# Cross-attention and quantised FFN on one core: two PSUM banks moved between the weighted values and the chunks, and all four engine orders rewritten

## The reference

```python
# x: 32 x 256 x 256, side and ctx: 32 x 256 x 256, mask: 32 x 16 x 256 x 256
z = layernorm(x)
k = concat(side @ Wk.T + bk, ctx @ Wgk.T + bgk)     # 512 keys
v = concat(side @ Wv.T + bv, ctx @ Wgv.T + bgv)
q = z @ Wq.T + bq                                   # 16 heads of 64
att = softmax(where(mask, -inf, q k' / 8))          # the mask covers the first 256 keys
x = x + (att @ v) @ Wo.T + bo
y = layernorm(x) / s_in -> bf16 -> float8 e4m3 -> @ quantised kernel * scales -> bf16 + bias
out = x + y
```

## Time and profile before

| | |
|---|---|
| runs | 2736.74, 2736.12, 2734.57 us |
| profiled execution, its own time | 2734.6 us |
| its span, first to last instruction | 2732.8 us |
| mean granted TensorE clock | 0.995 of full |
| TensorE busy | 2677.5 us (98%) |
| VectorE busy | 2163.6 us (79%) |
| GpSimd busy | 2048.8 us (75%) |
| ScalarE busy | 1859.6 us (68%) |
| chain that ended last | TensorE 80%, ScalarE 7%, issue 6%, VectorE 5% |
| HBM traffic | 74.8 MB, mean 27 GB/s |

### The profile page before, as it was taken

The page is one execution under the profiler, slowest core; times in us unless marked ns, Lnnn a source line. Parts: engine busy times, 40 slices in busy tenths (PEclk is TensorE's granted clock), DMA queues, the critical chain, the costliest instruction groups (busy, mean ns, idle before and its releaser), DMA issues.

```text
span 2732.8 us, 66539 instructions
## 1 busy us (share of the span) xinstructions
PE 2677.5 (98%) x20352; PEld 2349.6 (86%) x20352; DVE 2163.6 (79%) x5329; ACT 1859.6 (68%) x4454; POOL 2048.8 (75%) x2503
## 2 busy tenths in 40 slices
PE   5999999999999999999999999999999999999996
PEld 4888888888888888888888888888888888888885
DVE  5888777888778887778877788887788877788875
ACT  4766667766667666677666676666776666776664
POOL 4787777877777877777877778777788777787774
PEclk9999999999999999999999999999999999999998
DMA  3000000001000000000000000000000100000100
GB/s 144 24 24 24 27 27 23 27 19 31 23 27 27 27 19 27 27 23 27 19 31 23 27 27 27 19 27 27 26 24 19 31 27 24 26 27 19 31 16 8
DMA packets 57246, 75.18 MB, mean 28 GB/s; under 512 B 4992, under 2 KB 39296, under 8 KB 57216
## 3 DMA queue, kind: packets, MB, share of 16 engines
q1 hardware_dynamic: 57216, 74.81, 9.0%
HBM read 66.40 MB, written 8.39 MB: 27 GB/s over the span
## 4 chain that ended last, share of the span: by engine, by line
PE 80%; ACT 7%; issue 6%; DVE 5%; DMA 0%; SPq 0%; POOL 0%; DVEq 0%; ACTq 0%; POOLq 0%
PE ps_misc L603 28%; PE ps_scores L685 15%; PE ps_o L712 15%; PE ps_pt L697 13%; PE ps_misc L653 8%; ACT probs L875 3%; DVE probs L1144 2%; ACT pt_hi L882 2%; DVE pt_lo L1155 2%; ACT kv_out L852 1%; DVE o_t L1163 1%; PE ps_misc L662 1%; PE ps_misc L632 0%; DMA probs<-wv_t_dram 0%; ACT q_hi L840 0%
## 5 line engine op out<-in xcount | busy, mean ns | idle before, releaser
L477 POOL TENSOR_SCALAR probs<-probs,recips 128x512 f32<-128x512 f32 x1024 | 729.7, 723 | 330.2 <-DVE recips L1151 324.2
L875 ACT ACTIVATE probs<-probs,neg_max 128x512 f32<-128x512 f32 x1024 | 739.7, 725 | 214.8 <-DVE neg_max L1144 205.4
L1144 DVE CUSTOM_DVE_ANT_1 probs<-ps_scores,mask_sb 128x512 f32<-128x512 f32 x960 | 636.2, 685 | 217.9 <-PE ps_scores L685 177.6
L882 ACT CAST pt_hi<-ps_pt 128x512 fp32r<-128x512 f32 x1024 | 565.6, 589 | 306.7 <-PE ps_pt L697 300.0
L1155 DVE TENSOR_TENSOR pt_lo<-ps_pt,pt_hi 128x512 fp32r<-128x512 f32 x1024 | 675.6, 683 | 108.1 <-ACT pt_hi L882 107.0
L697 PE MATMUL ps_pt<-ident,probs 128*128 128x128 f32 x4096 | 554.2, 274 | 6.1 <-POOL probs L477 3.7
L712 PE MATMUL ps_o<-pt_hi,v_hl 128*128 128x256 f32 x2048 | 548.6, 302 | 3.0 <-DVE pt_lo L1155 3.0
L712 PE MATMUL ps_o<-pt_lo,v_hl 128*128 128x256 f32 x2048 | 508.1, 282 | 0.0
L697 PEld LDWEIGHTS ps_pt<-ident,probs 128*128 128x128 f32 x4096 | 457.3, 141 | 46.8 <-issue 35.5
L712 PEld LDWEIGHTS ps_o<-pt_hi,v_hl 128*128 128x128 f32 x2048 | 387.0, 189 | 62.0 <-issue 58.0
L712 PEld LDWEIGHTS ps_o<-pt_lo,v_hl 128*128 128x128 f32 x2048 | 389.3, 190 | 0.0
(11 more groups left out here) (105 smaller groups left out, 5846.1 us busy)
## 6 DMA issues: line engine op xcount, KB each, us to landing
mask_sb<-mask_dram SPq DMA_DIRECT2D x128, 256.0 KB, 3.1
x_sb<-x_dram SPq DMA_DIRECT2D x32, 256.0 KB, 2.7
side_raw<-side_t_dram SPq DMA_DIRECT2D x32, 256.0 KB, 3.8
scr_b<-ctx_t_dram SPq DMA_DIRECT2D x32, 256.0 KB, 2.7
out_dram<-y SPq DMA_DIRECT2D x32, 256.0 KB, 2.1
probs<-wq_t_dram SPq DMA_DIRECT2D x1, 1024.0 KB, 5.0
o_t<-wk_t_dram SPq DMA_DIRECT2D x1, 1024.0 KB, 7.3
wo_sb<-wgk_t_dram SPq DMA_DIRECT2D x1, 1024.0 KB, 9.3
```

The source lines that it names most:

```text
L477: nc.gpsimd.tensor_scalar(p, p, recips[:, h % RING, t:t + 1], 1.0, ALU.mult, ALU.mult).then_inc(norm_done, 1)
L875: nc.scalar.activation(p, p, ACT.Exp, bias=neg_max[:, h % RING, t:t + 1], scale=-1.0, accum_out=sums[:, h % RING, t:t + 1]).then_inc(exp_d ...
L882: nc.scalar.copy(pt_hi[:, h % 2, 2 * k:2 * k + 2, :], ps_pt[:, k, :, :]).then_inc(pthi_done, 1)
L1144: V.tensor_tensor_reduce(out=p, in0=s, in1=mask_sb[:, row::MASK_ROWS - row, :], scale=MASK_STEP, scalar=SCORE_LIMIT, op0=ALU.add, op1=ALU.min,
```

## The change

The weighted values get one bank, the chunks three; the wait of outputs moves from the add of the last head but one to that of the last head. GpSimd's semaphore for the split of the side and context rows becomes two, one for each. The four lists are rewritten: each has the same steps as before (TensorE 89, ScalarE 95, VectorE 122, GpSimd 72) in another order. SyncE's list is the same.

```diff
-MISC_BANKS = 2
+MISC_BANKS = 3
...
-        ps_o = psum("ps_o", [P, 2, 512])
+        ps_o = psum("ps_o", [P, 512])
...
-                if some(c.head(h) - 1):
-                    pe.wait_ge(o_done, c.head(h) - 1)
+                if some(c.head(h)):
+                    pe.wait_ge(o_done, c.head(h))
...
-                        last = mm(ps_o[:, h % 2, 0:S], v_hl[:, n % 2, kt, i, :], pt[:, h % 2, kt, :],
+                        last = mm(ps_o[:, 0:S], v_hl[:, n % 2, kt, i, :], pt[:, h % 2, kt, :],
...
-                    nc.scalar.copy(o_lo[:], ps_o[DK:P, h % 2, 0:S]).then_inc(olo_done, 1)
+                    nc.scalar.copy(o_lo[:], ps_o[DK:P, 0:S]).then_inc(olo_done, 1)
...
-                    V.tensor_tensor(dst, ps_o[0:DK, e, 0:S], o_lo[:], ALU.add).then_inc(o_done, 1)
+                    V.tensor_tensor(dst, ps_o[0:DK, 0:S], o_lo[:], ALU.add).then_inc(o_done, 1)
```

More of the change, by code:

```diff
@@ L438, in split_rows @@
                 wait_apart(pool, "pool", loaded, 16 * n)
-                nc.gpsimd.tensor_scalar(kv_hi[:, :, keys], raw, 1.0, 0.0, ALU.mult, ALU.add).then_inc(kvhi_done, 1)
-                pool.wait_ge(kvhi_done, 2 * (n - 1) + part + 1)
+                nc.gpsimd.tensor_scalar(kv_hi[:, :, keys], raw, 1.0, 0.0, ALU.mult, ALU.add).then_inc(kvhi_done[part], 1)
+                pool.wait_ge(kvhi_done[part], n)
                 nc.gpsimd.tensor_tensor(kv_lo[:, :, keys], raw, kv_hi[:, :, keys].bitcast(F32),
@@ L756, in batch @@
                 outputs(c, 3)
-                transposes(c, 4, 0)
-                transposes(c, 4, 1)
+                transposes(c, 5, 0)
+                transposes(c, 5, 1)
                 chunk(c, "v0", 2)
                 chunk(c, "k1", 2)
-                transposes(c, 5, 0)
+                chunk(c, "v1", 2)
+                outputs(c, 4)
+                chunk(c, "q", 3)
                 scores(c, 8, 0)
[L763 to L766, removed]
+                outputs(c, 5)
                 transposes(c, 6, 0)
                 transposes(c, 6, 1)
-                chunk(c, "q", 3)
                 chunk(c, "k0", 3)
+                scores(c, 8, 1)
+                chunk(c, "xq_prev", 0)
+                chunk(c, "k1", 3)
                 transposes(c, 7, 0)
-                outputs(c, 5)
                 transposes(c, 7, 1)
@@ L790, in batch @@
                 transposes(c, 10, 0)
+                outputs(c, 9)
                 transposes(c, 10, 1)
-                outputs(c, 9)
                 scores(c, 12, 1)
@@ L795, in batch @@
                 transposes(c, 11, 0)
+                outputs(c, 10)
+                scores(c, 14, 0)
                 transposes(c, 11, 1)
-                scores(c, 14, 0)
-                outputs(c, 10)
                 chunk(c, "k0", 0)
@@ L807, in batch @@
                 outputs(c, 12)
+                chunk(c, "k1", 0)
                 scores(c, 16, 0)
-                chunk(c, "k1", 0)
+                outputs(c, 13)
                 transposes(c, 14, 0)
@@ L813, in batch @@
                 scores(c, 16, 1)
-                outputs(c, 13)
+                transposes(c, 15, 0)
                 outputs(c, 14)
-                transposes(c, 15, 0)
                 transposes(c, 15, 1)
@@ L1225, in batch @@
-                attended(c, 0)
                 mins(c, 4, 0)
                 mins(c, 5, 0)
+                o_adds(c, 0)
+                pt_los(c, 1, 1)
+                attended(c, 1)
+                mins(c, 4, 1)
+                recip(c, 3)
                 pt_los(c, 2, 0)
                 pt_los(c, 2, 1)
-                attended(c, 1)
+                o_adds(c, 1)
+                mins(c, 5, 1)
                 moments_y(c)
-                mins(c, 4, 1)
-                o_adds(c, 0)
-                mins(c, 5, 1)
+                split_los(c, "q", 2)
```

243 lines of the change are left out of this document (120 added, 123 removed).

## The result

| | before | after |
|---|---|---|
| median us | 2735.69 (4 runs, 2734.57 to 2736.74) | 2768.65 (4 runs, 2766.69 to 2769.93) |
| ratio | 1 | 1.0120, 95% interval 1.0102 to 1.0137 |
| profiled execution, own time | 2734.6 | 2769.8 |

The change makes the kernel slower by 33 us, 1.2%. I had forecast slower by 12; the measured time lies just outside my range.

A forecast was written before the change was run, and what follows sets the result against it. TensorE was taken as the bound in all 30 middle batches. 82.81 + 0.82 + 0.10 = 83.73 us a batch against 83.34, +0.4 in each of 30, 12 us: median 2736.1 to 2748, range 2731 to 2768.

The forecast's parts named there:

- TensorE's bare steps, 82.81 a batch: TensorE's steps in the new order, laid end to end without waits, would take 82.81 us a batch.
- the 0.10 that I kept: TensorE's many stalls of 0.01 us, 0.10 a batch before the change, were assumed to stay.
- Transposes (12, 1) and outputs 11 behind scores (14, 0) have 0.1 to spare.: On TensorE around heads 11 to 14, these steps would not be late, with 0.1 us of slack.
- The third bank: Chunk-end-to-refill distance would be 2.6 us at the batch's first chunk, over 3.7 elsewhere; the bank wins 0.07 at most.
- All of these cost nothing: Moves in other queues, including the residual copy 15 us later, would cost nothing, with cover of 5 us or more.
- GpSimd and VectorE stretch each other here and there by 0.4, which my spacings leave out.: Said in support of the rival that the single bank costs at more places; stretches of 0.4 us were not counted.
- The place where one values bank fails, 0.82: Between scores (8, 1) and (10, 1), outputs 7 would be 0.51 us late and scores (10, 1) 0.82 in all.
- my lower bound of 0.4: Least cost between scores (8, 1) and (10, 1), from VectorE's own work never waiting for ScalarE: 0.4 us late.
- The rule on rotating banks: Skill's rule, speaking against one values bank; forecast held that other steps cover the evacuation in 15 of 16 heads.
- The third: Rival: single bank costs at more places, two of heads 5, 7, 9, 13 losing 0.4 each: 2772 us; chance 0.15.
- the forecast chain: ScalarE's row, then VectorE's add, reciprocal and minima, delaying scores (10, 1) by 0.82 us a batch, bounds 0.4 to 1.2.

The follow-up runs named there:

- best3: mins14_copyx_kvlo with head 6's lower copy before exp (9, 1), reciprocal 9 behind minimum (11, 0), GpSimd's rstd and head 9's second normalisation earlier: 2723.81 us.
- nocopyx: mins14_copyx_kvlo with GpSimd's residual copy put back where the changed kernel has it, behind head 7's first normalisation: 2745.45 us.
- mins14_copyx_kvlo: Changed kernel with head 14's first minimum and exp later, residual copy behind head 4's normalisation, v0 2's low part behind head 7's second normalisation: 2736.53 us.
- chain_short_norm9: mins14_copyx_kvlo with head 6's lower copy before exp (9, 1), x's moments and reciprocal 9 later, head 9's second normalisation earlier: 2749.30 us.
- copyx_early: Changed kernel with only GpSimd's residual copy moved, from behind head 6's normalisation to behind head 4's: 2759.36 us.
- old_banks: Changed kernel's new orders with the old bank numbers, two for the weighted values and two for the chunks: 3086.11 us.

## Why the prediction was wrong

- *TensorE's bare steps, 82.81 a batch.* Held, within about 0.2: best3 comes to 83.03 with no step more than about 0.05 late. The small stalls come to 0.22 there and 0.12 in the changed kernel, against the 0.10 that I kept.
- *"Transposes (12, 1) and outputs 11 behind scores (14, 0) have 0.1 to spare."* **This step failed**, by 0.71 a batch, nearly half of the 1.55 that stands where I had laid out nothing. I laid out the minimum of (14, 0) at 1.16 after its scores, and did not ask what else it waits for. I had looked at the waits that the diff edits, and not at those of the ring of four, whose text is unchanged but whose release (transposes (11, 1)) the new list moves behind its user. VectorE stands idle for 2.28 us just there, so its share of busy time would not have shown this wait.
- *The third bank: "over 3.7 at all others", and "wins 0.07 at most".* **Failed.** I measured the distance from a chunk's end to the refill of its bank; for q 3 to k1 3 it is over 5 us. What counts is when VectorE's list reaches the emptying: behind the quantising, the copy of v1 2 and the add of head 5. The wait is 0.66. As the prediction itself put it, TensorE would not be seen waiting for a chunk's bank; it is, 32 times.
- *"All of these cost nothing" (the residual copy moved by 15 us).* **Failed.** I followed its DMAs and SyncE's queue, where it indeed costs nothing, and left out the copy's own time on GpSimd, put into a stretch in which that engine has hardly a hole (94% busy from 1340 to 1356): 1.5 us of work, which the meetings with VectorE's quantising steps make 2.8. nocopyx prices it at 9 us once the other waits are gone; in the changed kernel it shows as 0.20 at transposes 8 and as a part (0.33) of the wait of k1 3, and these overlap, so they are not to be added to other prices.
- *"GpSimd and VectorE stretch each other here and there by 0.4, which my spacings leave out."* Left out wrongly: one such stretch, 0.6 longer than in the kernel before, was what made q's low part late.
- *The place where one values bank fails, 0.82.* The chain exists, step by step, but was mis-sized: 0.45 in mins14_copyx_kvlo, near my lower bound of 0.4. The lower copy came 0.2 earlier than laid out, mainly since from the third exp's start to the transposed copies of head 7 it is 0.71, not 0.84, and the bare distance to scores (10, 1) is 7.53, not 7.43. And its cause was only in part the bank, which holds up outputs 7 by 0.30; scores (10, 1) come equally late with two banks, because of VectorE's order. In the changed kernel none of it is seen, since the two earlier waits put TensorE behind the chain: scores (10, 1) come 8.28 after (8, 1), as forecast (8.25), for other reasons. A number that fits is no proof of its mechanism.
- *The rule on rotating banks.* In the total one bank cost nothing over two (3086.48 against 3086.11), and best3 has one bank and no late outputs; the other steps between all outputs give VectorE the time to empty it. Where VectorE was late, in chain_short_norm9, outputs 9 did wait for it. The Trainium skill, "Perfetto Trace Analysis", section "Matmuls", wants the evacuation of one group to overlap the next group's matmuls in another bank; by these runs it need not be so when other steps cover the evacuation.
- *Rivals.* The third had the sign and nearly the size (2772), but its mechanism, more heads' copies late, took no part in the changed kernel: none of its outputs waited for the add of the head before. In the edited kernels those of head 7 did, once the rest was mended, and in chain_short_norm9 those of head 9. That 2772 is near 2768.65 is luck.

In one sum: 82.81 + 0.66 + 0.20 + 0.69 + 0.12 = 84.48. Mending the two places takes 32 us off and gives about the time of the kernel before; the forecast chain, 0.45, is what then keeps the new lists from their gain of 0.3 a batch.

## What to carry to other kernels

When orders are rewritten, go over every wait of every moved step, above all those whose text the diff does not touch: a ring's reuse is late when its release has moved. For a bank's refill, date the step that empties it in its own engine's queue, not the distance on TensorE. Where an engine has no hole, an instruction moved in can cost its full length, and more where it meets another engine's step, at the next thing that others wait for, and mending one wait shows the next: only edits tried together tell what they are worth.

## What the runs showed of the hardware

**VectorE and GpSimd hold each other up, nearly for whole instructions.** VectorE's step with two SBUF inputs, 0.68 us alone, took 1.71 and, in `copyx_early`, 1.51; GpSimd's subtraction, 1.29 alone, took 1.74 when it was second. VectorE and GpSimd of `copyx_early`:

```profile
1340.04 1.51 DVE L1035 SCALAR_TENSOR_TENSOR scr_b<-scr_a 128x512 f32<-128x512 f32 x1
...
1342.69 0.68 DVE L1037 SCALAR_TENSOR_TENSOR xq<-scr_b,scr_a 128x512 bf16<-128x512 f32 x1
```

```profile
1339.72 1.28 POOL L470 TENSOR_TENSOR v_hl<-kv_out,v_hl 128x512 fp32r<-128x512 f32 x1
...
1342.79 1.74 POOL L470 TENSOR_TENSOR k_lo<-kv_out,k_hi 128x512 fp32r<-128x512 f32 x1
```

Here the first to start keeps its length; the second ends 0.55 after the first's end (1341.00 to 1341.55) on VectorE and 1.16 after it (1343.37 to 1344.53) on GpSimd, so it did nearly all its work behind the other. The Trainium skill, "SBUF — State Buffer", section "SBUF: two separate sides", calls the port pair that these two engines share an exclusive lock, held by whichever starts first for the whole instruction; these rows agree. The second instruction of the changed kernel's residual copy does not agree, by its recorded start: it starts 0.29 before VectorE's step (1344.77 against 1345.06), in all middle batches 0.29 to 0.30, and yet it is the one that is stretched, 1.56 us against 0.75 (the median in the kernel before), while VectorE's step keeps its 0.67. What decides there is open. VectorE's steps that read PSUM were not stretched: no masked minimum of `copyx_early` took over 0.70 us, beside whatever step of GpSimd.

**The clock gives a part of the price of a long wait.** `old_banks` has waits of over 2 us, and behind the one shown here the matmuls start 0.21 apart where they were 0.12 apart. Its TensorE, then windows (columns as in the earlier trace rows; the clock is the number before the last two):

```profile
1537.87 0.58 PE L603 MATMUL ps_misc<-wv_hi,kv_hi 128*128 128x256 f32 x1 [2.34 <-DVE q_lo L1050]
...
1538.46 0.41 PE L603 MATMUL ps_misc<-wv_lo,kv_hi 128*128 128x256 f32 x1
1538.67 0.41 PE L603 MATMUL ps_misc<-wv_hi,kv_hi 128*128 128x256 f32 x1
```

```profile
1540.00:1545.00 5.00, 5.00 (x28) 5.00 (x28) 2.60 (x5) 2.64 (x6) 0.76 (x2) 0.59 0.00 0
1545.00:1550.00 5.00, 5.00 (x42) 4.33 (x40) 3.17 (x9) 3.25 (x10) 3.87 (x5) 1.00 0.00 0
```

TensorE ran at the lower level, 1.2 GHz, for some microseconds and then at 2.4 again. Over the middle batches of `old_banks` chunk v0 0, behind this wait, took 1.80 to 2.73 us instead of 1.53; k1 1, behind one as long, 1.52 to 2.20, so it did not come every time. The changed kernel, whose waits in the repeating batch are under 0.7 us, shows a clock of 1.00 in both windows.
